# A transformer block on one core: in heads that begin with query products the maxima's scores come a unit later, projected tiles and keys behind the transposed maxima

## The reference

```python
h = layernorm(x) * (1 + ca) + sa
q = (h @ q_w.T + q_b)                      # 16 heads of 32
k, v = h @ k_w.T + k_b, h @ v_w.T + v_b    # one key and one value head for all
scores = q k / sqrt(32), causal; attn = softmax(scores); out = attn v
x = x + ga * (out @ o_w.T + o_b)
h = layernorm(x) * (1 + cb) + sb
x = x + gb * ffn(h)     # two Hadamard transforms, silu(gate) * up, 512 -> 2048 -> 512
```

## Time and profile before

| | |
|---|---|
| median of 3 runs | 2013.88 us (2007.88 to 2016.58) |
| the profiled execution's own time | 2008.55 us |
| its span | 2006.7 us |
| granted TensorE clock, mean | 0.99 |
| PE busy | 1932.6 us (96%) |
| DVE busy | 1387.0 us (69%) |
| ACT busy | 860.4 us (43%) |
| POOL busy | 243.2 us (12%) |

### The profile page before, as it was taken

The page is one execution under the profiler, slowest core; times in us unless marked ns, Lnnn a source line. Parts: engine busy times, 40 slices in busy tenths (PEclk is TensorE's granted clock), DMA queues, the critical chain, the costliest instruction groups (busy, mean ns, idle before and its releaser), DMA issues.

```text
span 2006.7 us, 31329 instructions
## 1 busy us (share of the span) xinstructions
PE 1932.6 (96%) x10816; PEld 1506.7 (75%) x10816; DVE 1387.0 (69%) x3296; ACT 860.4 (43%) x1615; POOL 243.2 (12%) x589
## 2 busy tenths in 40 slices
PE   6899999999999999889999999999999999999998
PEld 3566666666666556546788788999999999999997
DVE  5777777777767556675566887677676777767755
ACT  3366565555556554465222443332333323333221
POOL 2111113211321112112110010010010100101000
PEclk8899999999999999999999999999999999999999
DMA  7443344334433455554545988779788797787884
GB/s 228 126 110 76 91 124 111 101 81 112 118 101 76 140 172 164 176 171 144 194 137 210 370 314 342 289 289 344 280 300 335 289 344 291 295 334 283 325 308 163
DMA packets 116309, 424.32 MB, mean 211 GB/s; under 512 B 28076, under 2 KB 33452, under 8 KB 101944
## 3 DMA queue, kind: packets, MB, share of 16 engines
q1 hardware_dynamic: 104488, 371.92, 55.4%
q10 hardware_dynamic: 11664, 50.40, 6.7%
HBM read 318.16 MB, written 61.10 MB: 189 GB/s over the span
## 4 chain that ended last, share of the span: by engine, by line
PE 45%; DVE 5%; ACT 2%; DMA 1%; issue 1%; SPq 0%; POOL 0%; DVEq 0%; ACTq 0%
PE banks L1781 22%; PE banks L1872 15%; PE banks L1651 7%; DVE ln_stats L1218 1%; PE banks L1747 1%; PE banks L1741 1%; DMA upgate_items_dram<-items_ring 1%; DVE x_normed L1230 0%; DVE y L1343 0%; DMA upgate_raw<-in_w_ug 0%; ACT silu_gate L880 0%; ACT y_split L865 0%; ACT L880 0%; ACT L886 0%; DVE out_sb L1415 0%
## 5 line engine op out<-in xcount | busy, mean ns | idle before, releaser
L1872 PE MATMUL banks<-d_ring,y_split 128*128 128x512 f32 x1536 | 379.0, 393 | 1.9 <-DVE y_split L1363 1.9
L973 ACT ACTIVATE probs<-banks 128x512 f32<-128x512 f32 x576 | 312.4, 601 | 56.5 <-PE banks L1918 53.3
L1872 PEld LDWEIGHTS banks<-d_ring,y_split 128*128 128x128 f32 x1536 | 282.8, 189 | 57.2 <-DVE y_split L1363 2.1
L1781 PE MATMUL banks<-h_t_split,items_ring 128*128 128x256 f32 x2280 | 321.1, 283 | 1.9 <-DVE both L1320 1.9
L1781 PEld LDWEIGHTS banks<-h_t_split,items_ring 128*128 128x128 f32 x2280 | 298.9, 191 | 14.0 <-ACT h_t L791 4.0
L1941 PE MATMUL banks<-probs,v_ones 128*64 128x512 f32 (+3 forms) x1536 | 279.1, 498 | 3.0 <-POOL probs L1083 3.0
L1705 PE MATMUL banks<-k_stack,q_stacks 96*128 96x512 f32 (+3 forms) x768 | 251.8, 372 | 16.0 <-ACT neg_max_rows L742 5.7
L1918 PE MATMUL banks<-q_stacks,k_stack 98*128 98x512 f32 (+3 forms) x768 | 250.8, 369 | 6.2 <-ACT probs L973 4.3
L1941 PEld LDWEIGHTS banks<-probs,v_ones 128*64 128x64 f32 x1536 | 118.5, 137 | 162.8 <-issue 135.2
L1781 PE MATMUL banks<-input_sums,items_ring 128*128 128x256 f32 x1710 | 236.2, 283 | 0.0
L1083 POOL TENSOR_SCALAR_AFFINE_SELECT probs<-probs 128x128 f32<-128x128 f32 x512 | 146.9, 310 | 695.7 <-ACT probs L973 695.4
(11 more groups left out here) (179 smaller groups left out, 2283.7 us busy)
## 6 DMA issues: line engine op xcount, KB each, us to landing
items_ring<-upgate_items_dram SPq DMA_DIRECT2D x94, 1792.0 KB, 7.3
d_ring<-down_split_dram SPq DMA_DIRECT2D x128, 512.0 KB, 8.0
q_stacks<-q_split SPq DMA_DIRECT2D x192, 128.0 KB, 2.5
o_group<-o_raw SPq DMA_DIRECT2D x128, 128.0 KB, 2.4
upgate_raw<-in_w_ug SPq DMA_DIRECT2D x32, 512.0 KB, 4.4
upgate_items_dram<-items_ring ACTq DMA_DIRECT2D x8, 1792.0 KB, 7.4
upgate_items_dram<-items_made ACTq DMA_DIRECT2D x8, 1792.0 KB, 6.9
x<-in_x SPq DMA_DIRECT2D x32, 256.0 KB, 3.1
```

The lines of the kernel that those rows point to most:

```text
L973: nc.scalar.activation(pr[:, u, :], score_bank[:, at % SLOTS_SCORE, :], ACT.Exp, scale=SCALE).then_inc(exped, 1)
L1781: last = nc.tensor.matmul(item_bank(g, item), weights[:, a, item, k * P:(k + 1) * P], by_key(item_input(blk, item, m))[:, k, :], start=(k ...
L1872: last = nc.tensor.matmul(acc[:, t, :], ys[s][:, a, t * P:(t + 1) * P], dr[g % D_RING][:, m, :], start=(f == 0 and a + m == 0), stop=(f == ...
```

## The change

In heads that begin with query products (`begin` not empty) the keys `("max", H + 2, i)` go to units 0, 2, 3, 4, 5, 6, 7, 8, 8 instead of 0 to 8, and `top` to unit 3 instead of 2. In heads n = 5 the first projected tile goes from unit 2 to unit 3. Wherever a projected tile shares its unit with `top` (n = 5 to 8) it comes behind it, not ahead of it. In heads n = 13 the first `kv` goes from ahead of `top` in unit 2 to behind it in unit 3, and its stacking from unit 3 to unit 4.

```diff
-OUT_TILES = {5: {2: 0, 6: 1}, 6: {2: 2, 6: 3}, 7: {2: 4, 6: 5}, 8: {2: 6, 6: 7}}
+OUT_TILES = {5: {3: 0, 6: 1}, 6: {2: 2, 6: 3}, 7: {2: 4, 6: 5}, 8: {2: 6, 6: 7}}
...
-STACK_UNITS = (3, 7)
+STACK_UNITS = (4, 7)
+LATER_MAXIMA = (0, 2, 3, 4, 5, 6, 7, 8, 8)
...
-        units[TOP_UNIT].append(("top", H + 1))
+        units[TOP_UNIT + (1 if begin else 0)].append(("top", H + 1))
     if 0 < H < heads - AHEAD:
         for i in range(NS):
-            units[i].append(("max", H + AHEAD, i))
+            units[LATER_MAXIMA[i] if begin else i].append(("max", H + AHEAD, i))
...
         for u, t in OUT_TILES.get(n, {}).items():
-            units[u].insert(0, ("out", b - 1, t))
+            units[u].insert(1 if units[u][0][0] == "top" else 0, ("out", b - 1, t))
...
         if n == KV_STEP:
-            units[2].insert(0, ("kv", b + 1, 0))
+            units[3].insert(1, ("kv", b + 1, 0))
             units[5].insert(0, ("kv", b + 1, 1))
```

## The result

The changed kernel took 2020.59 us in the median of 10 runs (2014.03 to 2023.06), beside 2011.79 us (2007.88 to 2016.58, 10 runs) for the kernel before: a ratio of 1.0041, 95% interval 1.0029 to 1.0054, so +8.2 us (5.8 to 10.9). It is slower, within the half per cent that was called the same, and inside the range of 2006 to 2021. The forecast median of 2014.6 was 6 us too low, outside the "some 4 us" that went with it, and where +0.75 us was forecast, +8.2 was measured.

A forecast was written before the change was run, and what follows sets the result against it. PE, 96% busy and in order, was taken as the bound, so each term is a wait. Terms -0.8 + 0 + 0 - 1.6 + 2.7 + 0.45 = +0.75 us took the median from 2013.88 to 2014.6; range 2006 to 2021.

The forecast's parts named there:

- if the heads together change by more than 5 us: Over all heads: a sign, named beforehand, that the prediction is wrong; it forecast +0.75 us.
- tiles in begun heads: Heads 21, 37, 53: the last maxima score waits for a reduction behind the second tile; +0.9 us each, +2.7 in all.
- folds: Begun heads 49 and 57: the fold gets its bank ahead of the transpose, ending a 0.98 us wait; -0.8 each, -1.6.
- the collision: Heads 23, 24, 39: DVE's negation of maxima collides with POOL's bias sum, delaying transpose and tile; +0.65 us each, +1.95.
- where the start waits: Start of plain begun heads: transpose at 1.84 us, same bank as before; maxima score 2 still held to 2.34.
- m5 0.6 behind it: Begun heads, behind the first weighing: DVE takes the reduction of maxima score 5 0.6 us behind that of score 4.
- plain, rows and keys heads: Begun heads without tiles or folds: plain -0.2 us each, -0.8 in all; with rows 0; with keys 0.
- 22, 38, 54: Tile heads following a begun head that ends 0.9 us later, so the negation is done in time; -0.25 us each, -0.75.
- 40, 55, 56: Tile heads where the negation isn't late: the tile's short wait goes; -0.25 us each, -0.75.
- The transpose ahead of the tile waits for late maxima: Rival: the negation is late in all nine unbegun tile heads, 1.15 us each; +10.4, 2024.3 us; chance 0.11.

The follow-up runs named there:

- e8: Changed kernel with the second projected tile of heads n = 5 in unit 7 instead of 6: 2016.38 us, ratio 1.0031.
- e5: Changed kernel with POOL's first bias sum in tile heads behind the mask of unit 1, not ahead of unit 0's: 2019.58 us, ratio 1.0040.
- e1: Kernel before, with only the projected tiles of heads n = 6 to 8 moved behind the transposed maxima: 2019.98 us, ratio 1.0042.
- after: The changed kernel in its first profile, nothing else changed: span 2018.7 us; median of its 10 runs 2020.59 us, ratio 1.0041.
- e3: Changed kernel with the scores for maxima 3 and 4 exchanged: 2016.86 us, ratio 1.0029.
- e4: Changed kernel with the begun heads' maxima scores at units 0, 2, 3, 4, 4, 5, 6, 7, 8: 2015.52 us, ratio 1.0025.
- after again: The changed kernel profiled a second time, nothing changed: span 2014.7 us.

## Why the prediction was right, and where it was not

The outcome was right as a class and in range, but with luck. It lies 0.4 us inside the upper bound. Of the prediction's own signs of being wrong one came true, "if the heads together change by more than 5 us": they changed by 8.1. And the forecast median began at 2013.88, the median of three runs; of all ten it is 2011.79, from where +0.75 would have given 2012.5. Term by term:

- *Held: tiles in begun heads.* +0.9 each forecast, +0.89 measured; the wait of m8 was 0.90, the weighing 5.51 behind the tile where 5.5 was forecast, and e8 takes just this away.
- *Held in the sum: folds.* -1.6 against -1.43; in head 49 PE's 0.98 on the copied transpose has become 0.28. But -0.8 was forecast for each: head 49 won 1.08 and 57 only 0.35, where two new waits for DVE's half of a fold (L1215) of 1.12 and 0.90 us stand against the 1.07 and 0.97 of before. That the two make up for each other is luck.
- *Held: the collision.* The late negation in 23, 24 and 39 costs +0.87, +0.85 and +0.63 (0.65 forecast), the tile comes at 2.48 (2.47), and e5 removes it. DVE's negation ends 0.02 us behind POOL's sum in head 23, and in head 40 the second instruction, with two inputs in SBUF, was held for 1.22 us instead of 0.17. Who came first decided there: DVE reaches that instruction at 0.51, POOL's sum began at 0.39, 0.41 and 0.45 where it was held (e1, after, e3), and at 0.51, 0.55 and 0.61 where it wasn't (e8, e4, after again). The lock-out that the Trainium skill states (SBUF — State Buffer, "Who interferes with whom") was the right rule.
- *Held: where the start waits.* The transpose in head 17 is at 1.82, m2 at 2.34, both as before.
- *Failed: "m5 0.6 behind it".* It was 0.84. This step, m5's time behind m4, is in all plain, rows and keys heads, where -0.8, 0, 0 came out as +0.65, +1.09, +0.79. Of these 3.3 us e3 gives back 1.9, and so much is shown. The pitch was read from plain reductions, whose rows fit each other and not a pair in which the second goes on with the first one's maximum. The rest is other steps: e3 leaves +0.12 and +0.18 in heads with rows and keys (the transposes still wait for m6, 0.34 in both), and in plain heads it wins 0.08 and not 0.2. There the first weighing was to come at 3.2 instead of 3.75; it comes at 3.36 instead of 3.85, and by the start of the next head 0.08 is left.
- *Failed: 22, 38, 54.* 22 and 38 came out as -0.12 and -0.14, but 54 at +0.67 and not -0.25. *And 40, 55, 56*: 40 is chance (above). In 54, 55 and 56 I counted no fold: behind m4 the fold of unit 4 waits for m2's reduction, and m2 stands behind the tile on DVE. PE came there earlier, so its wait grew (in 55 from 0.44 to 0.92 us), and the tile itself came 0.2 later behind the transpose. In 54 about half is one more collision (below). Together with 22, 38 and 40 this is the 3.5 us that the two last rows of tile heads are over the forecast. No run moved the fold, but in heads 54, 55 and 56 of all 13 profiles it starts 0.75 us behind the end of DVE's addition of the residual (L1202), so it hangs on DVE's queue there.
- *Left out: the clock.* The forecast has no term for stretches at half clock, which go with most of the spread of some 8 us between runs of one kernel. For the changed kernel's median they hardly count, for e5's they do.

The collision in head 54 is that of POOL's second sum with DVE's addition of the residual, which takes 0.69 us in 55 and 56. Before and after the change (POOL from 782.27 and from 790.16), with the fold:
```profile
782.74 1.36 DVE L1199 TENSOR_TENSOR x_and_residual<-x_and_residual 128x512 f32<-128x512 f32 x1
784.85 1.10 PE L1735 MATMUL banks<-fold_again,hadamard 128*128 128x512 f32 x2 [1.11 <-DVE max_all L1125]
```
```profile
790.31 1.68 DVE L1202 TENSOR_TENSOR x_and_residual<-x_and_residual 128x512 f32<-128x512 f32 x1
792.73 1.10 PE L1738 MATMUL banks<-fold_again,hadamard 128*128 128x512 f32 x2 [1.90 <-DVE max_all L1128]
```

Of the rivals none came out whole. "The transpose ahead of the tile waits for late maxima" is the nearest to what happened (2024.3), and its mechanism is at work in 23, 24, 39 and, by chance, 40, but not in all nine heads.

What accounts for the time: outside half clock the heads sum to +8.1 for the changed kernel (about +7.5 in its second profile), and the time is +8.2 (5.8 to 10.9). What stays open: e3's heads (+6.4), which are 0.4 us above its interval at equal clock, about what a sum over heads scatters by; why the clock falls more often in the new orders; and what holds the negation in head 38.

## What to carry to other kernels

Moving independent work into a gap pays only what the gap's releaser doesn't also hold; what is owed comes back at a place with less cover, so follow each moved item to where it now stands, with its buffer's former user and its engine's order. A distance between two instructions read from the trace belongs to a pair with the same dependence: look whether the second reads what the first writes, and what used to lie between. And when one edit shifts the phase of the whole, a collision of two other engines may go from one head to the next: heads 22 to 24 and 38 to 40 gained or lost 0.9 us each by edits made elsewhere.

## What the runs showed of the hardware

- A DVE instruction that continues a running maximum, and waits for the semaphore of the plain reduction that wrote it, starts 0.84 us behind that reduction; behind one that writes another column it starts after 0.60.
- POOL's sum of 128x512 (1.29 us) held a DVE tensor_scalar of 128x8 till it ended, for up to 1.30 us instead of 0.17 (0.94 in head 23 of the changed kernel), a scalar_tensor_tensor with two SBUF inputs for 1.22 instead of 0.17, and a tensor_tensor of 128x512 with two SBUF inputs for 1.68 instead of 0.69. In the profile this is a longer duration of DVE's row and no wait. In the cases looked into, POOL's sum had begun first.
- The granted clock fell from 2.4 to 1.2 GHz for 3.4 us at a time, 1 to 5 times in an execution of one and the same kernel. In head 59 it did so in all seven executions of the table; in the kernel before PE was busy there for 5.08 of 6.00 us. A stretch costs 1.3 to 1.7 us.
